# Reordering the products with V in the attention blocks of a gated cross-attention and feed-forward kernel

## What is computed

```python
q = layernorm(x) @ Wq.T;  k = ctx @ Wk.T;  v = ctx @ Wv.T     # 16 heads of 32
scores = q @ k.T * 32**-0.5        # key j is seen by query i only if i >= j
out = softmax(scores) @ v
x = x + tanh(g_xattn) * (out @ Wo.T)
h = silu(layernorm(x) @ wg.T) * (layernorm(x) @ wu.T)         # 1536 wide
x = x + tanh(g_ffn) * (h @ wd.T)
```

## Time and profile before

| | |
|---|---|
| runs, us | 859.17, 857.37, 859.15 |
| median | 859.15 |
| profiled execution, its own time | 858.88 |
| its span in the profile | 857.1 |
| TensorE busy | 838.4 us, 98% of the span |
| VectorE, ScalarE, GpSimd busy | 681.9, 471.1, 415.8 us |
| granted TensorE clock, mean | 0.997 of full |

### The profile page before, as it was taken

How to read it: one execution, slowest core, us unless ns; L and a number is a source line. 1 busy time by engine, 2 the same in 40 slices (tenths; PEclk the granted TensorE clock), 3 DMA queues, 4 the chain that set the end, 5 groups by cost and what they waited for, 6 DMA issues and landing times.

```text
span 857.1 us, 12731 instructions
## 1 busy us (share of the span) xinstructions
PE 838.4 (98%) x3959; PEld 692.0 (81%) x3959; DVE 681.9 (80%) x1089; ACT 471.1 (55%) x1160; POOL 415.8 (49%) x374
## 2 busy tenths in 40 slices
PE   8999999999999998999999999999999999999997
PEld 6677888888888877788888888888888888888886
DVE  5998888888888888658898877998787988787673
ACT  5786676858576767555236356056354264461450
POOL 4654556474655565339515627235456047231240
PEclk9999999999999999999999999999999999999999
DMA  9235647373739230765414265234445133243212
GB/s 337 77 88 183 203 128 229 104 249 101 246 102 304 74 137 26 264 226 182 182 64 151 105 221 179 92 129 141 164 164 213 43 129 136 98 171 137 86 44 100
DMA packets 60874, 128.77 MB, mean 150 GB/s; under 512 B 8085, under 2 KB 20885, under 8 KB 60821
## 3 DMA queue, kind: packets, MB, share of 16 engines
q1 hardware_dynamic: 59428, 126.01, 43.3%
q10 hardware_dynamic: 1392, 2.10, 0.7%
HBM read 99.93 MB, written 27.79 MB: 149 GB/s over the span
## 4 chain that ended last, share of the span: by engine, by line
PE 81%; DVE 8%; SPq 3%; ACT 3%; DMA 2%; issue 2%; POOL 1%; ACTq 0%; DVEq 0%
PE psum L1982 33%; PE psum L2042 20%; PE psum L1693 11%; PE psum L1774 8%; PE psum L1753 5%; SPq L461 3%; PE psum L1716 3%; PE psum L1761 1%; ACT e L850 1%; DMA gates<-g_ffn 1%; DVE x_t L1362 1%; DMA x_ln<-x 1%; DVE mx L1188 1%; DVE pT L1135 1%; DVE bn L1122 1%
## 5 line engine op out<-in xcount | busy, mean ns | idle before, releaser
L1982 PE MATMUL psum<-xv,ring 128*128 128x512 f32 x1344 | 309.4, 390 | 0.5 <-DVE c L1538 0.5
L1982 PEld LDWEIGHTS psum<-xv,ring 128*128 128x128 f32 x1344 | 251.4, 188 | 55.9 <-DVE c L1538 1.7
L2042 PE MATMUL psum<-w_d,hT 128*128 128x512 f32 x768 | 177.0, 389 | 0.0
L2042 PEld LDWEIGHTS psum<-w_d,hT 128*128 128x128 f32 x768 | 144.2, 188 | 30.1
L742 POOL TENSOR_TENSOR hT<-th,hT 128x512 fp32r<-128x512 f32 x48 | 71.6, 1492 | 187.8 <-ACT hT L1072 187.8
L590 POOL TENSOR_TENSOR e<-e,rden 128x616 f32<-128x616 f32 x64 | 77.6, 1217 | 117.3 <-DVE rden L1218 93.2
L850 ACT ACTIVATE e<-psum,nmx,q_scale 128x77 f32<-128x77 f32 x256 | 102.6, 425 | 5.0 <-DVE nmx L1194 4.8
L1774 PE MATMUL psum<-wo,aT 128*128 128x512 f32 x384 | 95.6, 398 | 0.9 <-DVE aT L1155 0.5
L742 POOL TENSOR_TENSOR hT<-c,hT 128x512 fp32r<-128x512 f32 x48 | 63.8, 1329 | 65.1 <-ACT hT L1072 65.1
L1040 ACT ACTIVATE a<-psum 128x512 f32<-128x512 f32 x48 | 28.7, 598 | 112.8 <-PE psum L1982 112.8
L1693 PE MATMUL psum<-xT,wq 128*128 128x512 f32 x360 | 88.2, 397 | 0.5 <-DVE qT L1155 0.5
(11 more groups left out here) (118 smaller groups left out, 1280.5 us busy)
## 6 DMA issues: line engine op xcount, KB each, us to landing
ring<-w_var SPq DMA_DIRECT2D x48, 896.0 KB, 4.6
w_var<-stage SPq DMA_DIRECT2D x12, 896.0 KB, 4.5
x_ln<-x SPq DMA_DIRECT2D x32, 256.0 KB, 3.6
x_res<-x SPq DMA_DIRECT2D x32, 256.0 KB, 4.6
x_mid<-x_res SPq DMA_DIRECT2D x32, 256.0 KB, 2.0
x<-x_mid SPq DMA_DIRECT2D x16, 512.0 KB, 5.8
acc<-x_mid SPq DMA_DIRECT2D x16, 512.0 KB, 6.1
out<-acc SPq DMA_DIRECT2D x32, 256.0 KB, 2.0
```

The lines of the kernel that those rows point to most:

```text
L1982: last = nc.tensor.matmul(psum[:, bank, :], stat, mov, start=start and j == 0, stop=j == len(terms) - 1, skip_group_check=not start)
L2042: last = nc.tensor.matmul(down_bank(h, t), hT[:, a, m, t // TT, (t % TT) * P:(t % TT + 1) * P], w_d[:, HH * h + m, :], start=m == 0 and a ...
```

## The change

`weigh_values` takes the groups in pairs. For groups 0 and 1 it first issues both `values_full`, then both `values_rest`; then the same for groups 2 and 3. Before, each group's two parts stood together (`values` calls one and then the other).

```diff
             def weigh_values(n, b, b_before, masked):
                 scores(n, 0, b, masked, (m_base(n) - 2, m_base(n)))
-                for m in range(G):
-                    values(m_base(n) + m, m, b_before, t_base(n))
+                for first in (0, 2):
+                    for m in (first, first + 1):
+                        values_full(m_base(n) + m, m, b_before, t_base(n))
+                    for m in (first, first + 1):
+                        values_rest(m, b_before, t_base(n))
```

## The result

| | before | changed |
|---|---|---|
| runs, us | 859.17, 857.37, 859.15 | 863.58, 863.84, 863.96 |
| median | 859.15 | 863.84 |
| profiled execution, its own time (span) | 858.88 (857.1) | 863.58 (861.8) |
| mean granted clock in it | 0.997 | 1.0 |

The changed kernel is slower: ratio 1.0062, 95% interval 1.0047 to 1.0078, a median 4.7 us higher. The forecast was 865.2 (862.0 to 868.2), 6.0 us higher. The direction and the range hold; 1.4 us of the forecast are missing, and the traces say where they are. (The difference itself is clear of the noise: the interval lies wholly above 1.)

What follows compares the result with a forecast made beforehand. TensorE, busy 98% of the span, was taken as the bound, so its standstills are lost time. Blocks 2 to 6, 1 and 7 add 5.39 + 0 + 0.71 = 6.1 us: 865.2 us, range 862.0 to 868.2.

Steps and rivals of the forecast that it cites:

- The read-out chain: From the start of rest(0) until full(2) can reuse the bank: 0.61 + 0.04 + 0.63 + 0.69 + 0.06 = 2.03 us.
- Blocks 2 to 6: TensorE standstill ahead of full(2): 0.94 + 1.09 + 1.13 + 1.06 + 1.06, plus 0.11 for block 4, 5.39 us more.
- Block 7: Bank read-out starts 0.26 us later, and rest(2) now runs behind full(3), 0.45 more: cost 0.71 us.
- the rival of absorbed standstills: Later waits of TensorE shrink by the new ones; three quarters absorbed gives 860.7 us, no measurable change; chance 0.07.
- Possible gain: 0: At rest(0), its wait for the low part of pR gets covered; no such wait was listed, so 0 us.
- In front of the scores the move costs nothing: Second pair, rest(2) and rest(3): rest(3) ends when it did relative to full(2), so 0 us.
- Block 1: "cost 0": At full(2), already waiting 1.99 us behind VectorE's `nmx` and low(0): it starts when it did, cost 0.
- a case inside the range: Block 1's fall of the clock doesn't come: one fall less gives 863.5 us.
- The rival of the falling clock: Clock falls after each new wait in blocks 2 to 6: 873.7 us; one or two falls, 867 to 868.6; chance 0.08.

Runs made afterwards that it cites:

- e4: Against the kernel before: rest(0) and rest(2) issued behind 3 of the 6 matmuls of the next full, half the move; median 860.0 us, ratio 1.0021.
- e2: Against the kernel before: only groups 0 and 1 regrouped, groups 2 and 3 as before; median 862.93 us, ratio 1.0052.
- e3: Against the kernel before: only groups 2 and 3 regrouped, groups 0 and 1 as before; median 860.82 us, ratio 1.0026.
- e7: Kernel before with VectorE's low(0) ahead of the layernorm statistics, in block 1 alone; median 856.96 us, ratio 0.9982 to before.
- e1: The changed kernel run again, unaltered, beside before; median 863.75 us, ratio 1.007.
- e8: The changed kernel run a third time, unaltered, beside before; median 864.55 us, ratio 1.0073.
- e5: Changed kernel with the first 6 score matmuls of tile 1 moved between rest(1) and full(2); median 861.72 us, ratio 1.0038 to before.
- e6: Kernel before, order kept, with the first 6 score matmuls of tile 1 moved between rest(1) and full(2); median 858.2 us, ratio 1.0.
- e9: Changed kernel with VectorE's low(0) ahead of the layernorm statistics in block 1; median 864.22 us, ratio 1.0075 to before.
- e10: Kernel before with low(0) ahead of the layernorm statistics in block 1, run again in another set; median 857.08 us, ratio 0.9992.

## Why the prediction was right, and where it was not

**The read-out chain.** 2.03 us from rest(0) to full(2), built from five rows of before. Measured 2.02 or 2.03 in four blocks and 2.12 in block 4. This was the core of the forecast, and e4 shows the same 2.03 for a place in between.

**Blocks 2 to 6.** Forecast 5.39, measured 5.25. Block 4 is 0.10 above its term, nearly all of it the longer last step of the chain, and block 6 0.29 below. In block 6 the V products themselves cost the forecast: from full(0) to the next scores, 7.48 us before (272.20 to 279.68) and 8.55 now (275.29 to 283.84); 0.3 of it was then given back before block 7. Most of that lies ahead of one projection: it starts 0.52 us after the transposes before it in the kernel before (293.36 and 293.88) and 0.32 us after them now (297.45 and 297.77). What it waits for, no row marks.

**Block 7.** Forecast 0.26 + 0.45 = 0.71. From full(0) to the next scores it took 8.60 before and 9.32 now, 0.72 more. The later waits didn't absorb it: the one of 1.42 us is still 1.42, and another even grew, from 0.35 to 0.50 us, which makes the 0.87 of the table. So the rival of absorbed standstills fell. That the sum of blocks 2 to 7 meets 6.1 to 0.02 is partly luck: block 6 is 0.29 below, and blocks 4 and 7 together are 0.26 above.

**"Possible gain: 0."** Right: before had no wait at `values_rest`, and e2 to e4, which differ in when rest comes, show no gain either.

**"In front of the scores the move costs nothing."** Wrong for the second pair by itself: e3 measured 1.5 to 1.7 us. It came out right in the sum only because the first pair's wait makes full(2) late enough that low(1) is ready.

**Block 1: "cost 0"**, for the reason that the standstill is equally long. The waits are as forecast (1.97 against 1.99). The prediction named only `nmx` ahead of low(0); 0.84 us of layernorm statistics stand between them too (low(0) starts at 68.07, `nmx` ends at 67.23), and those are what e7 moves. The step that failed is the sum against the profiled execution of before: I took its fall of the clock, 1.4 to 1.7 us, as a fixed part of the kernel and noted its absence only as a case inside the range. The runs showed that it comes in some executions of either order and not in others, 24 of 54 of before over the three sets and 5 of 14 of the changed kernel. By its time, 859.15, the median of the first three runs of before has it (a mean clock is known only for the profiled one, 0.997), and the three of the changed kernel don't. That accounts for the difference between 6.1 and the 4.7 measured: at like clock it is 6.06 (e1) and 5.93 (e8). Which kind the three runs would be was chance.

**The rival of the falling clock.** It stays up behind each of the new waits of 0.96 to 1.05 us in every profile of the changed order. The rule weighed for it (the Trainium skill, "TensorE: Matmul & The Clock Gate", section "A second HAM failure mode: psum-queue depth-cycling") says that the clock swings with small idle times between groups that cycle through PSUM banks; for waits of this length the traces don't agree: from 104 to 370 us the mean clock is 1.00 in every profile of the changed order.

## What to carry to other kernels

When two accumulators take turns, what matters is not the work between two uses of a bank but the work between the signal "bank full" and its next use: a matmul moved from behind that signal to before it takes away its whole cover. Work that is moved in to cover it has to be taken from somewhere: in e5 half of it stayed as a gain over blocks 2 to 6, in e6 nothing. Measure the read-out chain once (here 2.03 us from the last group's first matmul to the next user) and compare it with what is issued in that time. And before a difference of a few tenths of a per cent is explained, sort the executions by their mean clock: medians of three can be of different kinds, and shares of kinds need dozens of executions.

## What was not expected of the hardware

- The same 2 us standstill of TensorE, at the same place after the same work, is followed by a fall of the granted clock in some executions (24 of 54 of before, from 3 of 15 to 10 of 16 by chip; 5 of 14 of the changed order) and not in the others. What decides it isn't shown. In the profile of before the clock was at half, 1.2 GHz, for the most part of 69.5 to 73.5 us; the executions with a fall are 1.6 to 2 us longer (857.57 against 859.24; 863.36 against 865.32).
- With that standstill shortened from 1.99 to between 1.08 and 1.16 us, none of 43 executions had the fall (e5, e6, e7, e9 and e10; 27 of them in the set where before had it in 11 of 23), and none of the new waits of about 1 us in blocks 2 to 7 brought one in the profiles.
- A wait that the timeline doesn't mark can lie inside a group: e3's 12 matmuls took 0.15 to 0.4 us longer in blocks 3 to 6. The difference of two starts shows it, the list of waits doesn't.
